# A two-layer graph network on one core: copy units moved beside the keys and values, x1 from ScalarE's queue, eleven query tiles in the drain, four banks

## The reference

```python
h = relu(layernorm(x))
x = x + relu(segment_sum(w_e * (h @ W)[src], dst))             # layer 0
h = relu(layernorm(x))                                         # layer 1
Q, K, V = h @ Wq, h @ Wk, h @ Wv                               # 8 heads of 32
score = (Q[dst] * K[src]).sum / sqrt(32) + relu(ef @ W1 + b1) @ W2 + b2
alpha = segment_softmax(score, dst)
out = x + segment_sum(alpha * V[src], dst) @ Wo + bo
```

## Time and profile before

| what | us |
|---|---|
| median of three runs | 874.93 |
| the profiled execution | 874.82 |
| its span | 872.9 |
| PE busy / DVE busy / POOL busy / ACT busy | 686.4 / 570.7 / 503.1 / 473.2 |
| gathers of edge rows by POOL (196 instructions of 0.94 to 1.17) | 5.0 to 339.5 |
| 98 tiles of keys and values, 2.38 each | 401.4 to 637 |

### The profile page before, as it was taken

How to read it: one execution, slowest core, us unless ns; L and a number is a source line. 1 busy time by engine, 2 the same in 40 slices (tenths; PEclk the granted TensorE clock), 3 DMA queues, 4 the chain that set the end, 5 groups by cost and what they waited for, 6 DMA issues and landing times.

```text
span 872.9 us, 13157 instructions
## 1 busy us (share of the span) xinstructions
PE 686.4 (79%) x3704; PEld 532.6 (61%) x3704; DVE 570.7 (65%) x1673; ACT 473.2 (54%) x1385; POOL 503.1 (58%) x432
## 2 busy tenths in 40 slices
PE   1376888999999999856999999999941358888883
PEld 0244665666666677635878888888831246666662
DVE  5278887888888876302676655555578248888883
ACT  0437786788888888622434444444452547555520
POOL 5888888788888851027566666553021105777663
PEclk9997999999999999986999999999975579999998
DMA  7877999999999984836388988979779995556551
GB/s 227 266 259 231 306 318 314 315 343 342 345 347 339 341 271 153 284 110 208 119 284 293 298 280 296 300 254 325 270 214 289 249 348 162 169 191 200 181 174 49
DMA packets 122937, 224.00 MB, mean 257 GB/s; under 512 B 27461, under 2 KB 100800, under 8 KB 112882
## 3 DMA queue, kind: packets, MB, share of 16 engines
q1 hardware_dynamic: 75602, 148.73, 50.9%
q0 software_dynamic: 21280, 48.73, 18.8%
q10 hardware_dynamic: 25984, 25.69, 8.4%
HBM read 133.05 MB, written 102.76 MB: 270 GB/s over the span
## 4 chain that ended last, share of the span: by engine, by line
PE 56%; DVE 16%; DMA 12%; issue 6%; ACT 4%; POOL 3%; ACTq 1%; DVEq 0%; SPq 0%; POOLq 0%
PE bank L1000 48%; DMA q<-ringC 4%; DVE small L984 4%; DMA ringB<-x 3%; PE bank L1115 2%; DVE store L973 2%; ACT ringB L609 2%; PE bank L1096 2%; DVE ringA L964 2%; PE bank L1069 1%; DMA h<-ringB 1%; DVE pz L765 1%; PE bank L1175 1%; POOL ringA L456 1%; DVE small L786 1%
## 5 line engine op out<-in xcount | busy, mean ns | idle before, releaser
L456 POOL DMA_INDIRECT store<-h,slot_gather x98 | 134.5, 1372 | 117.6 <-PE bank L1115 65.9
L1000 PE MATMUL bank<-Wkv_sb,small 128*128 128x256 f32 x784 | 187.1, 382 | 1.7 <-issue 1.7
L1000 PEld LDWEIGHTS bank<-Wkv_sb,small 128*128 128x128 f32 x784 | 150.5, 192 | 22.5 <-issue 2.1
L1000 PE MATMUL bank<-Wo_sb,small 128*128 128x256 f32 x392 | 108.1, 400 | 45.5 <-DVE store L973 45.5
L876 DVE TENSOR_TENSOR work<-bank,msgs 128x256 f32<-128x256 f32 x98 | 41.3, 422 | 133.8 <-PE bank L1000 133.8
L506 POOL DMA_INDIRECT out_x<-store,out_scatter x98 | 97.2, 991 | 52.0 <-issue 36.9
L456 POOL DMA_INDIRECT ringC<-in_x,dst_gather x98 | 92.6, 945 | 44.8 <-issue 25.7
L664 ACT ACTIVATE ringA<-store,scores 128x32 f32<-128x32 f32 x392 | 87.1, 309 | 48.9 <-PE bank L1175 45.8
L1000 PE MATMUL bank<-Wq_sb,small 128*128 128x256 f32 x392 | 104.8, 391 | 8.9 <-ACT ringC L537 8.8
L637 ACT COPY store<-bank 128x256 f32<-128x256 f32 x98 | 36.5, 372 | 134.7 <-PE bank L1000 134.7
L1000 PEld LDWEIGHTS bank<-Wo_sb,small 128*128 128x128 f32 x392 | 68.9, 196 | 61.5 <-DVE small L984 36.0
(11 more groups left out here) (180 smaller groups left out, 1249.6 us busy)
## 6 DMA issues: line engine op xcount, KB each, us to landing
out_x<-bulk SPq DMA_DIRECT2D x32, 1152.0 KB, 10.3
bulk<-in_x SPq DMA_DIRECT2D x28, 1152.0 KB, 8.0
ringA<-q SPq DMA_DIRECT2D x14, 896.0 KB, 7.0
ringB<-x SPq DMA_DIRECT2D x14, 896.0 KB, 5.4
out_x<-ringC SPq DMA_DIRECT2D x9, 1152.0 KB, 9.6
ringC<-in_x SPq DMA_DIRECT2D x7, 1152.0 KB, 8.0
x<-ringB SPq DMA_DIRECT2D x14, 512.0 KB, 3.7
h<-ringB ACTq DMA_DIRECT2D x14, 512.0 KB, 9.3
```

The lines of the kernel that those rows point to most:

```text
L456: pool.indirect_dma_start(to, None, table, bass.IndirectOffsetOnAxis(ap=at, axis=0), **more).then_inc(landed, 16)
L1000: return nc.tensor.matmul(o, lhsT, rhs, start=start, stop=stop)
```

## The change

1. **Ramp.** The copy units of the edges stage are loaded, added to and stored two turns later (load in turn g instead of g-2), behind the small loads of the same turn. ACT runs one Sqrt at the start.
2. **Queries.** h2 of a tile is transposed 11 tiles after it (LAG), instead of two groups (14). In the drain the products alternate between PSUM banks 0 and 4, and the last group's queries go to a free part of ringC. SP loads the first two groups' queries before the row of the open runs is known, and patches that one partition afterwards (`open_to`). POOL fetches slots of four tiles before the open rows, instead of two.
3. **Units.** 24 instead of 21 units go with the keys and values, one or two per group (`units`); SP stores a unit, loads the next but one, and at the end of a group loads queries. Six units instead of nine are left for the accumulating loads, and none is filled in the attend stage.
4. **x1.** The first two groups of x1 are loaded from ACT's queue, after the masks' last use (`rb_free`).
5. **Four banks.** The last product uses banks 2 to 5 in turn; it waits for the addition of four tiles back, not two.

```diff
@@ -27 +27,3 @@
-MIDDLE = EARLY + 3 * G // 2
+LAG = J + 4
+LAST_Q = T - LAG - 1
+MIDDLE = EARLY + 24
...
@@ -253,0 +257,8 @@
+def q_bank(t):
+    return bank[0 if t > LAST_Q and (t - LAST_Q) % 2 else 4]
+def q_row(l, j):
+    return C(j if l == G - 1 else J + j)
@@ -260,0 +272,5 @@
+def units(g):
+    k = MIDDLE - EARLY
+    return range(EARLY + k * g // G, EARLY + k * (g + 1) // G)
@@ -350,2 +365,0 @@
-        if g + 2 < EARLY:
-            bulk_load(g + 2)
@@ -363,0 +378,2 @@
+        if 0 <= g < EARLY:
+            bulk_load(g)
@@ -367,2 +383,2 @@
-        if 0 <= g + 1 < EARLY:
-            bulk_store(g + 1)
+        if 0 <= g - 1 < EARLY:
+            bulk_store(g - 1)
@@ -387,0 +404,7 @@
+    sp.wait_ge(h1, T)
+    for i in range(2):
+        sp.wait_ge(st_q[i], 32)
+    for a in range(2):
+        q_in(a)
+    for a in range(2):
+        sp.wait_ge(ql[a], 16)
@@ -390 +412,0 @@
-    bulk_load(EARLY + 2)
@@ -392,2 +414,3 @@
-    for a in range(2):
-        q_in(a)
+    sp.dma_start(ringA[P - 1:P, :].rearrange("o (u d) -> o u d", d=D),
+                 q_d.rearrange("(t p) d -> p t d", p=P)[P - 1:P, 0:2 * J, :]).then_inc(open_to, 16)
+    bulk_load(EARLY + 2)
@@ -403,12 +426,11 @@
-    for u in range(EARLY, MIDDLE):
-        if (u - EARLY) % 3 < 2:
-            a = 2 + (u - EARLY) // 3 * 2 + (u - EARLY) % 3
-            if a < G:
-                sp.wait_ge(same_rdy, a - 1)
-                ends_in(a)
-                sp.wait_ge(qs, J * (a - 1))
-                q_in(a)
-        if EARLY < u < MIDDLE - 2:
-            bulk_load(u + 2)
-        bulk_store(u)
-    for u in range(MIDDLE, MIDDLE + 4):
+    for g in range(G):
+        for u in units(g):
+            bulk_store(u)
+            if EARLY < u < MIDDLE - 2:
+                bulk_load(u + 2)
+        if g + 2 < G:
+            sp.wait_ge(same_rdy, g + 1)
+            ends_in(g + 2)
+            sp.wait_ge(qs, J * (g + 1))
+            q_in(g + 2)
+    for u in range(MIDDLE, BULK + 1):
@@ -418,2 +439,0 @@
-        for u in ((), (MIDDLE + 6, MIDDLE + 7), (MIDDLE + 8,))[g] if 0 < g < 3 else ():
-            bulk_store(u)
@@ -425,7 +445,2 @@
-            if a == 0:
-                sp.wait_ge(pe_sm, 5)
-            need(sp, o4, J * (a - 1))
-            sp.dma_start(group(ringB, ab), edge_rows(x1_d, a)).then_inc(x4[ab], 16)
-        if g == 0:
-            for u in range(MIDDLE + 4, MIDDLE + 6):
-                bulk_store(u)
+                need(sp, o4, J * (a - 1))
+                sp.dma_start(group(ringB, ab), edge_rows(x1_d, a)).then_inc(x4[ab], 16)
...
@@ -488 +503 @@
-        if t == 2:
+        if t == 4:
@@ -513,0 +529,2 @@
+    act.wait_ge(pdve, 1)
+    nc.scalar.activation(ssum[0:1, 0:1], epsc[0:1, :], ACT.Sqrt)
...
@@ -532,2 +548,3 @@
-        def copy_q(l, lb, j):
-            act.wait_ge(qp, J * l + j + 1)
+        def copy_q(t):
+            l, j = t // J, t % J
+            act.wait_ge(qp, t + 1)
@@ -535 +552 @@
-                if j == lo:
+                if j == lo and l < G - 1:
@@ -537 +554 @@
-            nc.scalar.copy(C(J + j), bank[4][:, 0:D]).then_inc(q2, 1)
+            nc.scalar.copy(q_row(l, j), q_bank(t)[:, 0:D]).then_inc(q2, 1)
@@ -573,2 +589,0 @@
-            if j == 1 and on(3):
-                rows_out(q2, st_q[1], q_d, ringC, l3, 1, 1)
@@ -577,2 +592,2 @@
-            if j == 5 and on(2):
-                rows_out(q2, st_q[0], q_d, ringC, l2, 0, 1)
+            if j in (2, 5) and on(2):
+                rows_out(q2, st_q[j // 3], q_d, ringC, l2, j // 3, 0 if l2 == G - 1 else 1)
@@ -583,9 +598,7 @@
-            if on(2):
-                u = l2b * J + j
-                act.wait_ge(t2, J * l2 + j + 1)
-                need(act, qp, J * l2 + j - 1)
-                nc.scalar.copy(hT[u % 2], bank[3][:, 0:D].rearrange("p (c e) -> p c e", c=NC)).then_inc(hT2, 1)
-            if j == 0 and on(3):
-                copy_q(l3, l3b, J - 1)
-            if j > 0 and on(2):
-                copy_q(l2, l2b, j - 1)
+            t = J * g + j - LAG
+            if 0 <= t < T:
+                act.wait_ge(t2, t + 1)
+                need(act, qp, t - 1)
+                nc.scalar.copy(hT[t % 2], bank[3][:, 0:D].rearrange("p (c e) -> p c e", c=NC)).then_inc(hT2, 1)
+            if 0 < t <= T:
+                copy_q(t - 1)
@@ -653 +666 @@
-    for u in range(MIDDLE + 4, MIDDLE + 6):
+    for u in range(MIDDLE + 4, BULK + 1):
@@ -654,0 +668,3 @@
+    act.wait_ge(rb_free, 1)
+    for a in range(2):
+        act.dma_start(group(ringB, a), edge_rows(x1_d, a)).then_inc(x4[a], 16)
@@ -659,2 +674,0 @@
-        if t in (3, 5, 9):
-            fill(MIDDLE + {3: 6, 5: 7, 9: 8}[t])
@@ -884,4 +898,2 @@
-            if j == 2:
-                add_unit(EARLY + g + g // 2)
-            if j == 5 and g % 2:
-                add_unit(EARLY + g + g // 2 + 1)
+            if j in (2, 5) and j // 3 < len(units(g)):
+                add_unit(units(g)[j // 3])
@@ -939,2 +951,7 @@
-        for i in range(2):
-            sm.link(nc.vector.scalar_tensor_tensor(fwd, reach[i], carry[:, i:i + 1], fwd, o0, o1))
+        sm.link(nc.vector.scalar_tensor_tensor(fwd, reach[0], carry[:, 0:1], fwd, o0, o1))
+        ins = nc.vector.scalar_tensor_tensor(fwd, reach[1], carry[:, 1:2], fwd, o0, o1)
+        if is_max:
+            sm.link(ins)
+        else:
+            ins.then_inc(rb_free, 1)
+            dve.wait_ge(rb_free, 1)
@@ -973 +990 @@
-            nc.vector.tensor_tensor(store3[:, J * g + j:J * g + j + 1, :], bank[2 + u % 2][:, None, 0:D],
+            nc.vector.tensor_tensor(store3[:, J * g + j:J * g + j + 1, :], bank[2 + (J * g + j) % 4][:, None, 0:D],
...
@@ -1020,2 +1035 @@
-        def queries(g, b, j):
-            t, v = J * g + j, b * J + j
+        def queries(t):
@@ -1023 +1037 @@
-            need(pe, q2, t)
+            need(pe, q2, t if t <= LAST_Q + 1 else t - 1)
@@ -1025 +1039 @@
-                ins = mm(bank[4][:, 0:D], hT[v % 2][:, c, :], Wqsb[:, c, :],
+                ins = mm(q_bank(t)[:, 0:D], hT[t % 2][:, c, :], Wqsb[:, c, :],
@@ -1064,2 +1078,2 @@
-            if on(2):
-                t_h = J * l2 + j
+            t_h = t - LAG
+            if 0 <= t_h < T:
...
@@ -1072,4 +1086,2 @@
-            if j == 0 and on(3):
-                queries(l3, l3b, J - 1)
-            if j > 0 and on(2):
-                queries(l2, l2b, j - 1)
+            if 0 < t_h <= T:
+                queries(t_h - 1)
@@ -1122,0 +1135 @@
+                pe.wait_ge(open_to, 16)
@@ -1164 +1177 @@
-            need(pe, o4, t - 1)
+            need(pe, o4, t - 3)
@@ -1166,2 +1179,2 @@
-                mm(bank[2 + v % 2][:, 0:D], aT[v % 2][:, c, :], Wosb[:, c, :], start=(c == 0), stop=False)
-            mm(bank[2 + v % 2][:, 0:D], ones[:, :], bo_part[:, :], start=False).then_inc(wo, 1)
+                mm(bank[2 + t % 4][:, 0:D], aT[v % 2][:, c, :], Wosb[:, c, :], start=(c == 0), stop=False)
+            mm(bank[2 + t % 4][:, 0:D], ones[:, :], bo_part[:, :], start=False).then_inc(wo, 1)
```

More of the change, by code:

```diff
@@ L199, in gnn_program @@
         ql, end_in = sem2("q_loaded"), sem2("run_ends_in")
-        s_end, end_out, open_in, open_out = (sem(n) for n in (
-            "run_ends_ready", "run_ends_in_dram", "open_q_in", "open_q_in_dram"))
+        s_end, end_out, open_in, open_out, open_to = (sem(n) for n in (
+            "run_ends_ready", "run_ends_in_dram", "open_q_in", "open_q_in_dram", "open_q_in_ring"))
         same_rdy, qs, qc = (sem(n) for n in ("same_run_ready", "q_spread_in_psum", "q_spread_ready"))
         lag3, s_bo, s_reach = sem("dve_lag3"), sem("bo_parts_step"), sem("reach_of_carries")
+        rb_free = sem("masks_in_ringB_used")
         s_flag, x_ps, x_sb, s_sm, pe_sm, act_sm, al_ps, s_al = (sem(n) for n in (
@@ L387, in _ @@
             bulk_load(EARLY + 1)
+            sp.wait_ge(h1, T)
[5 more added lines that the diff above has]
+                sp.wait_ge(ql[a], 16)
             sp.wait_ge(open_in, 16)
             sp.dma_start(q_d.rearrange("(t p) d -> t p d", p=P)[:, P - 1, :], q_open).then_inc(open_out, 16)
+            sp.wait_ge(open_out, 16)
+            sp.dma_start(ringA[P - 1:P, :].rearrange("o (u d) -> o u d", d=D),
+                         q_d.rearrange("(t p) d -> p t d", p=P)[P - 1:P, 0:2 * J, :]).then_inc(open_to, 16)
             bulk_load(EARLY + 2)
-            sp.wait_ge(open_out, 16)
-            for a in range(2):
-                q_in(a)
             sp.wait_ge(x1r, T)
@@ L476, in edges @@
                         fetch(C(j), x, dg_i[:, t:t + 1], xd_in[j])
-                    if j == 3 and 0 <= g + 2 < EARLY:
-                        i, n = bulk_at(g + 2)
-                        if g == -2:
+                    if j == 3 and 0 <= g < EARLY:
+                        i, n = bulk_at(g)
+                        if g == 0:
                             pool.wait_ge(s_mlp, 144)
                         pool.wait_ge(bulk_ld[i], 16 * (n + 1))
-                        add_bo(None, g + 2)
+                        add_bo(None, g)
```

(18 more changed lines are left out.)

## The result

The changed kernel takes 820.04 us (median of four runs, 818.59 to 821.54), against 874.08 for the kernel before (four runs): a ratio of 0.9386, 95% interval 0.9352 to 0.942. The forecast was 809, with 796 to 834 as its range. The profiled execution takes 818.59 us, its span 816.8.

A forecast was written before the change was run, and what follows sets the result against it. Bounds were taken by stage: POOL in the edges, PE in keys and values, PE and DVE waiting for each other in attend. Ramp 16 + drain 10 - units 1 + attend 41 = 66; 874.8 - 66 = 809 us, range 796 to 834.

The forecast's parts named there:

- Ramp: Start of the edges stage: POOL sheds two additions and a 3.97 us wait, a 14.1 us lead; 16 us gained.
- the edges give little: Edges stage: DMA at 0.88, not POOL, sets the turn; ramp gives 5, drain 4; 826 us, chance 0.15.
- Drain: End of the edges stage: fewer query tiles and earlier loads, less extra gathers and traffic; about 10 us gained, bounds 2 and 16.
- Units: Keys and values stage: more copy units, additions hidden by PE, DMA lagging slightly; 1 us lost, between 0 and 8.
- x1: Before the attend stage: load issued at 672, landing 14 us later, 2 us of stall left; 18 us gained.
- the scatter floor: Attend stage: POOL's 98 scatters take 126 us and start only once all units are stored, at 694, ending at 820.
- Banks and scatter: Attend stage: 18 from x1 and 24 from four banks, replaced by one term limited by POOL's scatters; 41 us gained.

The follow-up runs named there:

- the short course: Runs of the changed kernel or its variants whose edges stage ends early, last W product near 339 us instead of 346.5; unedited, two of ten runs near 811 us.
- the quiet drain: Changed kernel with the store of copy unit 13 and loads of units 14 and 15 moved behind the patch of the open rows; 806.19 us, 0.9203.

## Why the prediction came out as it did

The sign, the range and the largest term were right; the forecast was 11 us too fast. By its own steps:

- *Ramp, 16 forecast, 10.7 measured.* POOL's lead in the ramp was right (gather 43 starts 13.6 us earlier, 14.1 forecast). The step that failed is "as POOL sets the turn, its lead reaches the end of the edges". Of the 13.6, about 1.3 went in the third turn, behind the stall of 5.7 us, and 1.8 in the last turns. The prediction hoped that such stalls would go; the additions, put later, still met DVE (5.32 and 5.70 us in the first two turns). On the short course the last gather starts at 320.1 to 320.9, 18 us before that of the kernel before, which is above the forecast; so the 10.7 depends on which course the profiled run took.
- *The rival "the edges give little"* had a point that the forecast passed over: its 0.88 is a mean over a stage whose first turns (0.82) and last (0.76) are lighter, and the steady part stands at 0.95 to 1.01. It was so in the kernel before (columns as in the earlier trace rows):

```profile
110.00:310.00 200.00, 180.55 (x1096) 131.95 (x1094) 160.29 (x604) 160.43 (x421) 161.42 (x132) 0.98 0.97 331
```

The rival was set aside because the turn equals POOL's own work; leaving out most of the additions showed that another bound lies at the same height. That it is the DMA engines is argued, not tested.
- *Drain, 10 forecast, 7.0 measured.* The tiles came as counted: from the last W product to the last query store 28.5 us before and 19.4 now, 9.1 against 10. The loads moved ahead gave 5.3 against 6. The term that was mis-sized is what was given back, 2.6 for two gathers and 3.5 for traffic: the gather of the open rows starts 10.8 us after the last query store instead of 3.4, 7.4 more. 9.1 + 5.3 - 7.4 = 7.0. The path was another one too: the sum follows the query tiles and the last query store, but the gather now stands behind four slot gathers, and these behind the last h2 store, which took 10.3 us to land. So shortening the chain of tiles gains little: three tiles alone are worth 1.9.
- *Units.* One us lost was forecast, 0.7 gained. DMA at 295 GB/s, and 327 with 27 units, holds nothing up.
- *x1.* 14 us to landing were forecast, 20.2 measured; the wait of 5.5 instead of 2 costs nothing, since POOL ends 10 us after DVE. That this term lies under the scatter floor the prediction said; that ACT's queue is worth 0.8 us it did not.
- *Banks and scatter, 41 forecast, 38.1 measured.* POOL was to start at 694 less the gain before, 18.4: 675.6. It started at 679.5, 3.9 later; the sum had 42.8 before it was put at 41, so this accounts for most of the difference. The pace of 1.29 and the end by POOL were right. The pair takes 2.5, not 2.7.

## What to carry to other kernels

When one term lies under a floor set by another engine (the scatters here), price the floor, and move what lets it start earlier: three more copy units out of the way were worth 9 us, the earlier issue of x1 on another queue under 1. Read the DMA share in the steady part of a stage, not over the whole of it, before naming one engine as the bound. Follow a wait to the store that really ends it: in the drain it was the h2 store, not the query store. And an order of work that moves a long POOL operation moves what it meets on DVE: look at what stands still beside it, in which turn, and at the first turns of several runs before trusting one profile.

## What the runs showed of the hardware beyond that

- Which small DVE instruction meets a POOL addition differs between executions of the same kernel (L781 at 72.12 in one profile, L779 at 94.70 in the other). A meeting of 5.7 us in an early turn goes with 7 us at the end of the stage, with PE's granted clock at 0.50 behind it, while stalls of 3 us in nearly every later turn stand in the faster traces. By the trace the blocked instruction's row begins 0.62 us before that of the addition it waited for (72.12 and 72.74), so an instruction is not safe because its row begins first.
- With the 16 DMA engines at 0.96 and a third query store per group, one issue held ACT for up to 2.95 us where another takes 0.37.
- A store of 384 KB landed 2.5 us after its issue in the quiet end of the drain before and 2.8 in the quiet drain; beside 3.5 MB of copy units it took 8.2 and 10.3.
